# Back-transposes, residual, norm and token transposes one FFN group earlier, and a mask row buffer per batch

## What is computed

```python
xn = _layernorm(x, axis=-1)                      # rows of x
q, k = _conv(y, wq, bq, mask_cond), _conv(y, wk, bk, mask_cond)
v = _conv(xn, wv, bv, mask)                      # 256 x 256 weights, standardised
scores = softmax(q @ k.T / SCALE)                # 8 heads of 32 x 32
out = _conv(scores @ v, wo, bo, mask) + xn
out = (out - mu) * rsqrt(var + EPS) * gamma + beta   # over channels
x = x + tanh(g_xattn) * out * mask
xr = _layernorm(x, axis=-1).reshape(-1, 1024)    # the tokens of the FFN
h = silu(silu(xr @ w1.T) @ w3.T) @ w2.T
x = x + tanh(g_ffn) * (top-2 gated sum of h, added into 8 rows of x)
```

## Time and profile before

| | before |
|---|---|
| median of 3 runs | 1243.17 us (1241.69 to 1245.37) |
| the profiled execution | 1245.78 us, its span 1244.0 us |
| TensorE busy | 1102.8 us, 89% of the span |
| VectorE busy | 842.8 us, 68% |
| ScalarE busy | 466.9 us, 38% |
| POOL busy | 387.2 us, 31% |
| chain that ended last | PE 42%, DVE 34%, ACT 10%, issue 9%, POOL 3%, DMA 1% |

### The profile page before, as it was taken

One profiled execution on the slowest core, in us unless ns is written; L12 is line 12 of the kernel. 1 busy time (PEld: TensorE's weight loads), 2 busy tenths in 40 slices (PEclk: granted clock), 3 DMA queues, 4 the chain that ended last, 5 costly groups with the idle time before them and its releaser, 6 DMA issues.

```text
span 1244.0 us, 18398 instructions
## 1 busy us (share of the span) xinstructions
PE 1102.8 (89%) x6871; PEld 646.5 (52%) x6871; DVE 842.8 (68%) x1951; ACT 466.9 (38%) x762; POOL 387.2 (31%) x404
## 2 busy tenths in 40 slices
PE   1656699899989999899989999899989999799998
PEld 1445455655556546554556546554556546555553
DVE  4589567975696758865696757875696757864322
ACT  3662434234234524244234524244234524234231
POOL 2281012550255113550255113550255113540000
PEclk9977699999999999899999999899999999899999
DMA  9601300041001500041001500041001500023000
GB/s 271 169 18 73 114 1 1 2 142 62 1 1 35 170 2 1 1 150 55 1 1 34 170 2 1 1 148 57 1 1 34 170 2 1 1 86 138 1 1 1
DMA packets 35214, 65.78 MB, mean 53 GB/s; under 512 B 1758, under 2 KB 19748, under 8 KB 35132
## 3 DMA queue, kind: packets, MB, share of 16 engines
q1 hardware_dynamic: 33660, 63.25, 15.8%
q10 hardware_dynamic: 1472, 1.31, 0.4%
HBM read 47.75 MB, written 16.81 MB: 52 GB/s over the span
## 4 chain that ended last, share of the span: by engine, by line
PE 42%; DVE 34%; ACT 10%; issue 9%; POOL 3%; DMA 1%; ACTq 0%; DVEq 0%; POOLq 0%
PE bank L608 26%; PE bank L479 6%; DVE ub L1067 5%; DVE act_t L1180 3%; DVE ub L1086 3%; ACT h_hi L815 3%; DVE xbuf L1109 3%; DVE h_lo L1185 3%; DVE ub L1082 2%; ACT ub L786 2%; DVE xt_lo L1161 2%; PE bank L533 2%; PE bank L488 2%; DVE bst L1103 2%; DVE bst L1022 2%
## 5 line engine op out<-in xcount | busy, mean ns | idle before, releaser
L608 PE MATMUL bank<-xt_hi,w1b 128*128 128x512 f16 x1024 | 328.2, 381 | 20.4 <-DVE xt_lo L1161 14.1
L608 PE MATMUL bank<-w3b,h_hi 128*128 128x512 f16 x1024 | 310.3, 385 | 2.8 <-DVE act_t L1180 2.8
L608 PE MATMUL bank<-w3b,h_lo 128*128 128x512 f16 x512 | 196.2, 383 | 0.0
L608 PE MATMUL bank<-xt_lo,w1b 128*128 128x512 f16 x512 | 195.1, 381 | 0.0
L1185 DVE SCALAR_TENSOR_TENSOR h_lo<-act_t,h_hi 128x512 f16<-128x512 f32 x128 | 125.7, 982 | 91.5 <-ACT h_hi L815 91.5
L1180 DVE SCALAR_TENSOR_TENSOR act_t<-act_t,bank 128x512 f32<-128x512 f32 x128 | 85.9, 671 | 133.5 <-ACT act_t L809 133.2
L809 ACT ACTIVATE act_t<-bank,fs 128x512 f32<-128x512 f32 x128 | 87.4, 683 | 234.4 <-PE bank L608 234.4
L608 PEld LDWEIGHTS bank<-xt_hi,w1b 128*128 128x128 f16 x1024 | 100.4, 98 | 135.0 <-DVE xt_lo L1161 13.6
L815 ACT ACTIVATE h_hi<-act_t 128x512 f16<-128x512 f32 x128 | 80.6, 630 | 219.7 <-DVE act_t L1180 219.7
L608 PEld LDWEIGHTS bank<-w3b,h_hi 128*128 128x128 f16 x1024 | 100.6, 99 | 73.8 <-DVE act_t L1180 4.2
L393 POOL TENSOR_TENSOR ub<-bo_b,mcur 128x2048 f32<-128x2048 f32 x16 | 57.6, 3600 | 202.2 <-DVE dg L1044 202.2
(11 more groups left out here) (189 smaller groups left out, 1946.6 us busy)
## 6 DMA issues: line engine op xcount, KB each, us to landing
xbuf<-in_x_dram SPq DMA_DIRECT2D x16, 1024.0 KB, 5.8
out_dram<-xbuf SPq DMA_DIRECT2D x16, 1024.0 KB, 4.7
x_lo<-in_ctx_dram SPq DMA_DIRECT2D x16, 512.0 KB, 5.9
mrow<-in_mask_dram SPq DMA_DIRECT2D x16, 512.0 KB, 4.5
w1b<-in_w_dram SPq DMA_DIRECT2D x8, 512.0 KB, 7.5
w3b<-in_w_dram SPq DMA_DIRECT2D x8, 512.0 KB, 7.4
xbuf<-in_w_dram SPq DMA_DIRECT2D x1, 4096.0 KB, 13.6
ub<-in_wq_dram ACTq DMA_DIRECT2D x1, 256.0 KB
```

Of the source, the lines that this page charges most:

```text
L608: mm = pe.matmul(bk[:, :], left, right, start=d == 0 and n == 0, stop=d == FT - 1 and n == 2)
```

## The change

It does three things.

1. `token_stages` gives 12 and 13 for every pair. `attention_back`, `residual` and its coefficients go from stages 10 and 11 to 9 and 10, `normed` of the second norm from 11 and 12 to 10 and 11. So these steps go with groups 10 to 14, and stage 14 holds only y's work.
2. mrow holds two rows, one for each batch of a pair, each with a semaphore. A row is loaded when the batch of the same place in the pair before has been served. SyncE's queue has other places for it: both rows of the first pair ahead of the weights, then each row behind the load of y of the same batch.
3. In stage 7 POOL does, after the coefficients of b = 0, the second half of `add_beta` of b = 0 (as before) and now also the first half of b = 1; stage 8 has the second half of b = 1 after its coefficients. Before, both halves of b = 1 came after them.

```diff
     def token_stages(j):
-        return (12, 14) if first_pair(j) else (13, 14)
+        return (12, 13)
...
-        mrow = sb("mrow", [P, T])
+        mrow = sb("mrow", [P, 2, T])
...
+        mrow_in = [sem(f"mrow_in{b}") for b in range(2)]
...
-            def load_mask(q):
-                need(sp, sm["xpre_ready"], q)
-                sp.dma_start(mrow[:, :], a["mask"][q, 0, :].partition_broadcast(P)).then_inc(sm["mrow_in"], 16)
+            def load_mask(q, b):
+                need(sp, sm["xpre_ready"], q - 1)
+                sp.dma_start(mrow[:, b, :], a["mask"][q, 0, :].partition_broadcast(P)).then_inc(mrow_in[b], 16)
...
             def pair(j, last=False):
                 load_x(j)
-                load_mask(2 * j + 1)
                 if not last:
-                    load_y(j + 1, 0)
-                    load_mask(2 * j + 2)
-                    load_y(j + 1, 1)
+                    for b in range(2):
+                        load_y(j + 1, b)
+                        load_mask(2 * j + 2 + b, b)
                 store(j)
...
-            load_mask(0)
+            for b in range(2):
+                load_mask(b, b)
             sp.wait_ge(sm["small_in"], SMALL)
...
-            load_mask(1)
-            load_y(1, 0)
-            load_mask(2)
-            load_y(1, 1)
+            for b in range(2):
+                load_y(1, b)
+                load_mask(2 + b, b)
             store(0)
...
                 if s in (7, 8):
                     b, q = s - 7, 2 * j + s - 7
                     if s == 7 and not first_pair(j):
-                        add_beta(q, b, 0)
+                        add_beta(j, 0, 0)
                     coefs(q, mvc, coc, TT, EPS * XS * XS, 1.0, "cn", (sm["v_ready"], TT * q), m1c[:, b, :])
+                    if s == 7 and not first_pair(j):
+                        add_beta(j, 0, 1)
+                        add_beta(j, 1, 0)
                     if s == 8 and not first_pair(j):
-                        add_beta(q, b, 0)
-                    if not first_pair(j):
-                        add_beta(q, b, 1)
-                if s in (10, 11):
-                    b, q = s - 10, 2 * j + s - 10
+                        add_beta(j, 1, 1)
+                if s in (9, 10):
+                    b, q = s - 9, 2 * j + s - 9
                     coefs(q, mv2, co2, CH, EPS, XS, "ln2", (sm["xs2_ready"], q))
...
-                elif s in (10, 11) and d % 2 == 0:
-                    attention_back(2 * j + b, b, d // 2)
+                elif s in (9, 10) and d % 2 == 0:
+                    attention_back(2 * j + s - 9, s - 9, d // 2)
...
-                if s in (11, 12):
-                    normed(2 * j + s - 11, s - 11, co2, sm["ln2_coef"], sm["xs2_ready"])
+                if s in (10, 11):
+                    normed(2 * j + s - 10, s - 10, co2, sm["ln2_coef"], sm["xs2_ready"])
...
-                if s in (10, 11):
-                    residual(2 * j + s - 10, s - 10)
+                if s in (9, 10):
+                    residual(2 * j + s - 9, s - 9)
```

More of the change, by code:

```diff
@@ L202, in build @@
         out_done = [sem(f"out_done{b}") for b in range(2)]
+        mrow_in = [sem(f"mrow_in{b}") for b in range(2)]
         y_in = [sem(f"y_in{b}") for b in range(2)]
-        names = """mrow_in w1a_in w1b_in w3a_in w3b_in small_in
+        names = """w1a_in w1b_in w3a_in w3b_in small_in
             ident_set s_zero sc_zero w_rows w_max w_all w_clamp w_bits w_scale w_tr w_hi w_lo wr_tr wr_hi wr_lo
@@ L363, in x_low, with add_beta @@
                 pool.tensor_tensor(x_lo[:, b], xs[b], x_hi[:, b], ALU.subtract).then_inc(sm["xlo_ready"], 1)
-            def add_beta(q, b, c):
+            def add_beta(j, b, c):
+                q = 2 * j + b
                 for n in (2 * c, 2 * c + 1):
@@ L369, in add_beta @@
                     if n == 0:
-                        pool.wait_ge(sm["mrow_in"], 16 * (q + 1))
+                        pool.wait_ge(mrow_in[b], 16 * (j + 1))
                         pool.wait_ge(sm["xs_ready"], q + 1)
@@ L375, in add_beta @@
                         pool.wait_ge(sm["mtmp_step"], 7 * q + 2 * n)
-                    pool.tensor_tensor(mtmp[:, :], mrow[:, h], gcol[:, 1, c:c + 1].broadcast_to([P, TC]), ALU.mult)\
+                    pool.tensor_tensor(mtmp[:, :], mrow[:, b, h], gcol[:, 1, c:c + 1].broadcast_to([P, TC]), ALU.mult)\
                         .then_inc(sm["mtmp_step"], 1)
@@ L398, in attention @@
                 if s in (1, 2) and first_pair(j):
-                    add_beta(s - 1, s - 1, 0)
-                    add_beta(s - 1, s - 1, 1)
+                    add_beta(j, s - 1, 0)
+                    add_beta(j, s - 1, 1)
                 if s in (7, 8):
```

## The result

| | before | changed |
|---|---|---|
| median | 1243.58 us (1241.69 to 1245.37, 4 runs) | 1223.72 us (1222.51 to 1226.55, 4 runs) |
| ratio | | 0.9844, 95% interval 0.9820 to 0.9868 |
| profiled execution, its span | 1245.78, 1244.0 us | 1224.83, 1222.9 us |
| pairs 0 to 6, first FFN matmul of the first to that of pair 7 | 985.1 us | 964.7 us |

The changed kernel is 19.9 us faster. The forecast was 12.4 us and 1230.8 us, with a range down to 1226.5: the sign was right, and the time fell out of the range on the fast side. One execution of the kernel before, in its last run, took 2901 us and is left out. In the changed kernel L546 is L549, L608 is L611, L786 is L789, and so on: three lines further down.

What follows compares the result with a forecast made beforehand. TensorE, busy 89% of the span, was taken as the bound, so only its waits could be won: 14.2 us removed - 3.4 new wait + 1.6 start = 12.4 us, giving 1230.8 us, range 1226.5 to 1237.5.

Steps and rivals of the forecast that it cites:

- Waits removed, 14.2 us: TensorE's waits at groups 0, 12, 14 and 15 (xt_lo, act_t, xbuf) go: 7.1, 3.0, 2.8 and 1.3 us.
- The new wait, 3.4 us: TensorE's back transposes of batch 1, group 11, wait for ScalarE's L786: about 0.55 us per pair; bounds 2.1 to 7.7 us.
- The part without POOL's lateness: Batch 1's back transposes reach L786's output too early even if POOL is never late: about 0.1 + 0.25 us.
- Beta times mask as the condition: POOL's second set in stage 7 makes coefficients 0.2 us late; batch 1's beta ends at 680.6, ahead of its residual (682.1).
- Mask rows and SyncE: A row buffer per batch and new queue order: no cost, up to 1.8 us if cover in the prologue fails.
- The start, 1.6 us: First pair: xt_lo begins at 141.86, not 144.19, less a 0.7 us shift; gain 1.6 us, bounds 0 and 2.3.
- the shift of 0.7 us: At the start, y's largest ends later on VectorE, so POOL's all-reduces come about 0.7 us later.
- rivals 1 and 5: 1: TensorE's loop-end gap takes back 5.9 us, 1236.7, chance 0.10; 5: gap shrinks up to 6.3 us, 1224.5, chance 0.04.
- (2): VectorE's backlog moves: waits for act_t and banks, 7.1 us, return at groups 12 and 13; 1237.9, chance 0.06.
- (4): Nothing gained: the waits at group 0 are TensorE's own start of a new weight set; 1243, chance 0.03.
- (3): POOL blocked beside attention_out, TensorE waits in group 11: 4.8 us per pair, 34 us in all; 1261, chance 0.04.
- the sum itself: Whole kernel: 14.2 - 3.4 + 1.6 = 12.4 us gained, giving 1230.8 us against the median.

Runs made afterwards that it cites:

- the stages alone: Kernel before with back transposes, residual, norm and tokens one group earlier, mask row buffer and beta times mask unmoved: 1243.0 us (ratio 0.9994).
- the second profiles: Both kernels run once more without edits: changed 1225.72 us (before beside it 1243.32); kernel before 1246.03 us in its profiled execution.
- the two kernels with half of stage 7 later: TensorE issues stage 7's last four of eight tiles behind group 8's own matmuls: 1217.89 us on the changed kernel, 1231.54 us on the kernel before.

## Why the prediction was right in sign and wrong in size

**Waits removed, 14.2 us: right.** Each is gone. The idle sums agree: 62.2 - 50.2 = 12.0 us saved, the new wait of 2.3 us included.

**The new wait, 3.4 us: right mechanism, one part too large.** VectorE and POOL in the pair read above:

```profile
662.16 0.54 DVE L1096 BATCH_NORM_AGGREGATE mvc<-bst 128x2 f32<-128x6 f32 x7
```

```profile
661.85 1.27 POOL L381 TENSOR_TENSOR xbuf<-xbuf,mtmp 128x512 f32<-128x512 f32 x1
663.08 0.20 POOL L333 TENSOR_TENSOR coc<-mvc,minus 128x8 f32<-128x8 f32 x1
```

L333 stands right behind L381 and 0.38 us behind mvc. In the kernel before it stood 0.16 us behind mvc (672.40 and 672.56), so POOL makes it 0.22 us late, and I had 0.2. TensorE waits once, 0.40 us in five pairs, 0.17 in the first and 0.10 in the last: 2.3 us. I had 0.55 a pair. The part without POOL's lateness is what I had too large: the two kernels with the stages moved and beta in its old place wait 0.18 us a pair, where I had 0.35.

**Beta times mask as the condition: missed.** I checked POOL only as a delay of the coefficients, and noted in half a sentence that beta of batch 1 ends ahead of its residual. I never priced the stages without it. The runs show that without it the stages save nothing (1242.7 and 1243.0 us).

**Mask rows and SyncE: right in the loop, about 0.8 us at the start.** In the loop nothing shows: 1242.7 us with the row buffer and 1243.0 without. At the start TensorE's wait for y's high part (L907) is 7.5 to 7.8 us in the six profiles with one mask row ahead of the weights, and 8.1 to 8.9 us in the seven with two. I had looked only at the weights behind the second row. What delays y's high part isn't traced.

**The start, 1.6 us: right mechanism, 0.7 us too small.** Read from the point where TensorE restarts on ScalarE's norm of u (first row: before, then changed):

```profile
123.03 1.12 PE L546 MATMUL bank<-ident,ub 128*128 128x128 f32 x4 [5.36 <-ACT ub L786]
124.68 1.11 PE L549 MATMUL bank<-ident,ub 128*128 128x128 f32 x4 [5.37 <-ACT ub L789]
```

```profile
141.79 0.37 POOL L356 PARTITION_ALL_REDUCE ms<-ms  x1 [6.75 <-issue]
```

From there to group 0 the kernel before takes 146.73 - 123.03 = 23.7 us and the changed one 146.10 - 124.68 = 21.4. In all thirteen profiles it is 23.6 to 23.9 us with the old stages and 21.2 to 21.5 with the new: 2.3 us gained. xt_lo follows the weight scale directly, at 143.57, as I had it. But the shift of 0.7 us that I took off did not come. POOL was free 0.75 us later, and the all-reduce still began 17.1 us after TensorE's restart in both kernels (140.09 - 123.03 and 141.79 - 124.68); it ranges from 16.9 to 17.2 us over all profiles. I had taken the idle 7.45 us ahead of it for a fixed length. Against the whole start the gain can't be told: group 0 starts 0.6 us earlier in the profile (146.10 against 146.73), five profiles with the start of the kernel before have it at 143.1 to 147.1 us, mean 146.2, and six with the changed start at 143.7 to 146.1, mean 145.1. They scatter ahead of the stages that moved: with the start of the kernel before TensorE's restart came at 119.4 us in one profile and at 123.0 to 123.3 in the other four.

**The rivals.** The loop gap neither grew nor shrank: five gaps of 1.05 to 1.43 us, 6.1 us in all, after 6.2 (rivals 1 and 5). VectorE's backlog did not come back as a wait of TensorE (2). Group 0's waits were what the trace said they were, and went (4). POOL was not blocked (3): the additions beside attention_out took 1.27 us, where the slow one of the stages alone, 1.78 us at 677.91, began 0.03 us after one of VectorE's L1185, which reads act_t and h_hi. The Trainium skill (SBUF — State Buffer, "Who interferes with whom") says that a VectorE instruction with two SBUF inputs contends with a GpSimd instruction that reads SBUF, and one with at most one doesn't, unless it runs in a 2-port mode. These rows agree.

**The step that failed is the sum itself.** It took the pairs of the profile before, removed idle time and left every other duration as it was. In those durations was a part that is no work: 16.8 us lost to TensorE's level of 1.2 GHz, after a wait that the change doesn't touch. I read that wait and not the clock behind it. What the changed kernel gained above the forecast in the pairs is 20.4 - 10.8 = 9.6 us: 7.0 from the clock in the first profiles, 12.0 - 10.8 = 1.2 from a smaller idle sum, and 1.4 left over, the column "left" of the account, which I can't name. With the second profiles the clock's part is 3.4 us, and by the two kernels with half of stage 7 later it is 20.4 - 14.5 = 5.9 or 17.0 - 14.5 = 2.5 us. So the term that I put at nothing without a reason measured 2.5 to 7.0 us, and how much of it the change itself makes stays open. With a term for it of nothing to 7 us, the range would have reached below 1223.7.

**What stays open.** What sets the place of the drop is not shown. The kernel before returns to PEclk 0.70 to 0.74 in all twelve stretches of two profiles; a shift of 0.86 us per pair in either direction cut its loss by 2 to 4 us. The changed one stood between 0.70 and 0.86. The share of DMA in the stretches goes with PEclk in pairs 1 to 5 of the changed kernel (0.02 at 0.70, 0.17 at 0.86), but not as its cause as far as one can see: the kernel before with half of stage 7 later has 1.00 with a DMA share of 0.01. That transfers begin sooner where TensorE gets on faster would explain it, and isn't shown.

## What to carry to other kernels

Before adding up removed waits, read the granted clock behind every wait that stays: time lost there is neither idle nor work, it came out different in nearly every kernel here whose loop had changed, and a forecast needs a term for it with both ends. An edit that brings a consumer forward can be worth nothing until its slowest producer, on whatever queue, is brought forward too; here two edits of next to no value each made 1.6% together. At a start that scatters, read a change from the last instruction ahead of it and not from zero. And where a lasting wait has a saturated engine behind it, rearranging the waiting engine returns little (5.8 us of the hoped 21 to 29); taking work off the saturated one was not tried.

## What the runs showed of the hardware

- The same wait of 5.9 us is followed by 1.4 to 3.0 us of loss at 1.2 GHz; one kernel repeats nearly the same value in every pair and from profile to profile (2.6 to 3.0), another doesn't.
- After a wait of 3.3 us the clock fell in four stretches of six and stayed at 2.4 GHz in two, in either of the two kernels that had it. After the wait of 2.7 us in their pair 0 it fell in both, 0.8 and 0.9 us behind the restart.
- Added or removed matmuls need not cost their duration in one profile. For 6.0 us of them in pairs 0 to 6 the kernel before took 1.7 us more, and 10.0 us less without as many. By the medians the three such edits cost or brought 5.0, 8.3 and 10.4 us for 6.9, and the intervals reach 6.9 in each.
- The first 123 us came out up to 3.9 us apart between five profiles in which these instructions are the same (the kernel before twice, and three edits of it that leave the start alone).
- POOL's all-reduce at the start began 16.9 to 17.2 us after the same restart of TensorE in thirteen profiles, whether POOL was free 7.4 or 6.7 us ahead of it.
